# Sorting each node tile's expert choices with a one-hot product and storing them as eight runs, in place of two indirect scatters

## The reference, cut to what matters

```python
N, D, H, E = 12500, 256, 512, 8                      # 212500 edges
msgs = layernorm(x)[src] * edge_weight[:, None]
agg  = segment_sum(msgs, dst, N)                     # dst is sorted
x    = x + agg @ W.T + b
xf   = layernorm(x)
probs = softmax(xf @ gate_w + gate_b)
top2_vals, top2_idx = top_k(probs, 2)
for e in range(E):                                   # weight is zero unless e was chosen
    out += cw[:, e] * (gelu(xf @ W1[e] + b1[e]) @ W2[e] + b2[e])
x = x + out
```

## Time and profile before

| | us |
|---|---|
| median of 3 runs (2953.14 to 2955.53) | 2954.43 |
| the profiled execution | 2958.51 |
| its span | 2956.7 |
| POOL busy in the span | 2013.2 |
| PE busy in the span | 2196.5 |
| DVE busy in the span | 1409.3 |

### The profile page before, as it was taken

The page is one execution under the profiler, slowest core; times in us unless marked ns, Lnnn a source line. Parts: engine busy times, 40 slices in busy tenths (PEclk is TensorE's granted clock), DMA queues, the critical chain, the costliest instruction groups (busy, mean ns, idle before and its releaser), DMA issues.

```text
span 2956.7 us, 40846 instructions
## 1 busy us (share of the span) xinstructions
PE 2196.5 (74%) x9206; PEld 1482.4 (50%) x9207; DVE 1409.3 (48%) x5982; ACT 740.5 (25%) x1985; POOL 2013.2 (68%) x2107
## 2 busy tenths in 40 slices
PE   3656755984876977966966877978877887776695
PEld 2433533653654655644644654655555555544463
DVE  8855434453453443453454453443555555454422
ACT  3410200330221332321321221322322222222242
POOL 6657777777777777777777777777777777751121
PEclk8777977897988988988988987989998899887798
DMA  9663433443444443445555444434455564542423
GB/s 337 225 237 115 127 116 115 136 126 121 129 139 123 133 126 122 139 147 163 173 165 163 145 131 132 132 118 125 138 168 161 161 194 148 158 131 85 151 86 109
DMA packets 231445, 432.24 MB, mean 146 GB/s; under 512 B 47020, under 2 KB 158542, under 8 KB 228006
## 3 DMA queue, kind: packets, MB, share of 16 engines
q0 software_dynamic: 100368, 275.72, 31.3%
q1 hardware_dynamic: 128246, 144.38, 15.4%
q10 hardware_dynamic: 2592, 9.45, 0.8%
HBM read 326.80 MB, written 102.56 MB: 145 GB/s over the span
## 4 chain that ended last, share of the span: by engine, by line
POOL 50%; issue 20%; PE 15%; DVE 11%; DMA 3%; ACT 1%; ACTq 1%; DVEq 0%; SPq 0%; POOLq 0%
POOL rows L363 40%; POOL slots L391 5%; PE bank L599 5%; POOL results L396 5%; PE bank L685 4%; PE bank L667 3%; DVE spread L976 1%; DMA results<-y_sb,result_i 1%; PE bank L676 1%; DMA got<-results 1%; DVE y_sb L1154 1%; DVE item_t L1124 1%; DVE square_n L1023 1%; DVE pre_bn L932 1%; DVE bn L955 0%
## 5 line engine op out<-in xcount | busy, mean ns | idle before, releaser
L363 POOL DMA_INDIRECT rows<-xhat,src_t x1536 | 1470.0, 957 | 476.4 <-issue 464.4
L599 PE MATMUL bank<-rows,spread 128*80 128x256 f32 x3328 | 910.2, 435 | 324.8 <-issue 160.1
L599 PEld LDWEIGHTS bank<-rows,spread 128*80 128x80 f32 x3328 | 564.1, 175 | 607.6 <-issue 320.4
L685 PE MATMUL bank<-w,hT 128*128 x1848 | 489.1, 411 | 115.3 <-ACT hT L822 66.9
L685 PEld LDWEIGHTS bank<-w,hT 128*128 128x128 f32 x1848 | 366.2, 205 | 229.1 <-issue 180.9
L667 PE MATMUL bank<-w,xiT 128*128 x924 | 452.0, 612 | 11.6 <-ACT xiT L805 2.2
L989 DVE TENSOR_TENSOR acc<-acc,bank 128x160 f32 x208 | 67.0, 322 | 755.4 <-PE bank L589 730.3
L396 POOL DMA_INDIRECT results<-y_sb,result_i x231 | 226.8, 982 | 237.4 <-DVE y_sb L1157 181.3
L976 DVE TENSOR_SCALAR spread<-iota_w,dst_rel,wgt 128x80 f32<-128x80 f32 x1536 | 378.5, 340 | 0.2
L1153 DVE CAST result_i<-xi 128x1 int32 x231 | 35.1, 152 | 620.6 <-PE bank L685 339.1
L822 ACT ACTIVATE hT<-bank,b1T 128x128 f32<-128x128 f32 x924 | 263.4, 367 | 217.8 <-PE bank L676 212.2
(11 more groups left out here) (159 smaller groups left out, 1755.3 us busy)
## 6 DMA issues: line engine op xcount, KB each, us to landing
xi<-slots SPq DMA_DIRECT2D x231, 136.0 KB, 2.7
got<-results SPq DMA_DIRECT2D x97, 256.0 KB
rows<-xhat,src_t POOLq DMA_INDIRECT x1536
x_t<-in_x SPq DMA_DIRECT2D x97, 128.0 KB
x_d<-x_t SPq DMA_DIRECT2D x97, 128.0 KB, 2.3
res<-x_d SPq DMA_DIRECT2D x97, 128.0 KB
out_nodes<-res SPq DMA_DIRECT2D x97, 128.0 KB
w<-in_x SPq DMA_DIRECT2D x12, 1024.0 KB, 12.7
```

What stands on the lines that cost most here:

```text
L363: pool.indirect_dma_start(rows[q][:, c, :], None, x if g < RAW else xhat, bass.IndirectOffsetOnAxis(ap=src_t[:, g * CG + c:g * CG + c + 1] ...
L599: done = nc.tensor.matmul(B_SUM[0:W, 0:D], spread[g % 2][:, c, :], rows[q][:, c, :], start=c == 0, stop=c == CG - 1)
L685: done = nc.tensor.matmul(B_Y[:, 0:D], hT[i % 2][:, j, :], w2[:, bass.ds(e, 1), j, :].rearrange("p o f -> p (o f)"), start=j == 0, stop=j ...
```

## The change

POOL no longer sends. For each tile, in the turns after its part is placed:

1. DVE (`mask_choices`, at the end of its turn) writes a one-hot matrix of 128 nodes by 256 places, where a place is the choice's rank when the tile's 256 choices are sorted by expert.
2. PE (`sort`, a turn later) multiplies it with the tile in two products of 128 places by 272 columns. They go to the bank that `linear` uses, the first behind `turn_sums`, the second behind `step_down`. ACT copies each out (`copy_sorted`), and `linear`, now behind `step_down`, waits for the second copy.
3. SP (a turn later) stores the 256 sorted rows in a staging array in DRAM (`store_sorted`).
4. SP (a turn later) loads sixteen addresses into registers at once and copies eight runs of 128 rows each, one for an expert, from staging to `slots` (`copy_runs`). A run is always 128 rows long, and what lies behind its end is overwritten by the next tile's run, so a tile's copies wait for those of the tile before.

`place` has five more small operations for the run starts, and loses the cast to `slot_i`. The ring of node sums falls from 16 tiles to 8. `xs` is cleared at the start. One tile in a turn is masked, in place of two or four sent; three items in a turn start once the last run is planned. The plan grows from 235 to 239 turns. By turn 150, 107 items have entered it where 116 had; by turn 207, when the last group is gathered, 186 where 192 had. The last tile is done in turn 222 where it was sent in turn 219.

```diff
-RING = 16
+RING = 8
+STAGE = 3 * P
+STAGES = 3
...
-        for _ in range(2 if busy else 4):
-            if send_next < NT and place_at.get(PART_OF[send_next], tau) < tau:
-                t.sends.append(send_next)
...
+        if turns:
+            t.sort, t.stage, t.runs = turns[-1].mask, turns[-1].sort, turns[-1].stage
+        if send_next < NT and place_at.get(PART_OF[send_next], tau + 1) <= tau:
+            t.mask = send_next
+            send_next += 1
+        if t.runs >= 0 and t.runs == PARTS[PART_OF[t.runs]][1] - 1:
+            sent_at[PART_OF[t.runs]] = tau
...
+            def store_sorted(t):
+                if t >= STAGES:
+                    sp.wait_ge(runs_in, 16 * NX * (t - STAGES + 1))
+                sp.wait_ge(sorted_ready, 2 * t + 2)
+                sp.dma_start(stages[t % STAGES][0:2 * P].rearrange("(h p) f -> p h f", p=P), sorted_x[t % 2][:]).then_inc(staged[t % STAGES], 16)
...
+                at = loaded_row(sp, run_ends[k % 2][:, j].rearrange("p c e -> p (c e)"))
+                sp.wait_ge(staged[t % STAGES], 16 * (t // STAGES + 1))
+                if t:
+                    sp.wait_ge(runs_in, 16 * NX * t)
+                if t in EPOCH_TILES[1:]:
+                    sp.wait_ge(tails_in, 16 * NX * EPOCH_OF[k])
+                for e in range(NX):
...
+                    sp.dma_start(slots[bass.ds(b, P), :], stages[t % STAGES][bass.ds(a, P), :]).then_inc(runs_in, 16)
...
+            def sort(t, h):
+                if h == 0:
+                    pe.wait_ge(mask_set, t + 1)
+                pe.wait_ge(x1_ready, n_linear[0])
+                if t or h:
+                    pe.wait_ge(sorted_ready, 2 * t + h)
+                nc.tensor.matmul(B_NODE[:, 0:XW], sort_mask[t % 2][:, h * P:(h + 1) * P], xs[:, t % XR, :],
+                                 start=True, stop=True).then_inc(sort_done, 1)
...
+            def copy_sorted(t, h):
+                act.wait_ge(sort_done, 2 * t + h + 1)
...
+                nc.scalar.activation(sorted_x[t % 2][:, h, :], B_NODE[:, 0:XW], ACT.Copy).then_inc(sorted_ready, 1)
...
+            nc.vector.memset(xs[:], 0.0)
...
+                nc.vector.tensor_scalar(first_choice[:], iota_s[:], at[0], None, op0=ALU.is_equal).then_inc(half_mask, 1)
+                dve.wait_ge(half_mask, t + 1)
+                nc.vector.scalar_tensor_tensor(sort_mask[t % 2][:], iota_s[:], at[1], first_choice[:],
+                                               op0=ALU.is_equal, op1=ALU.add).then_inc(mask_set, 1)
```

More of the change, by code:

```diff
@@ L119 @@
     refill: int = -1
-    sends: list = field(default_factory=list)
+    mask: int = -1
+    sort: int = -1
+    stage: int = -1
+    runs: int = -1
     steps: list = field(default_factory=list)
@@ L230, in build @@
     xhat = nc.dram_tensor("xhat", (N, D), F32, kind="Internal").ap()
+    stages = [nc.dram_tensor(f"stage{i}", (STAGE, XW), F32, kind="Internal").ap() for i in range(STAGES)]
     blocks = slots.rearrange("(n p) f -> n p f", p=P)
@@ L325, in tile, with loaded_row @@
             return acc[:, :, t % RING * P:(t % RING + 1) * P]
+        def loaded_row(eng, row):
+            return nc.values_load_multi_w_load_instructions(row, engines=(eng.engine,), skip_runtime_bounds_check_because="bounded where used")[1]
         def valid_rows(t):
@@ L385, in _ @@
             pool.wait_ge(src_rest, 16)
[L387 to L392, removed]
             def scatter_result(i):
@@ L527, in turns @@
                         refill(t.refill)
+                    if t.stage >= 0:
+                        store_sorted(t.stage)
+                    if t.runs >= 0:
+                        copy_runs(t.runs)
+                        k = PART_OF[t.runs]
+                        if t.runs == PARTS[k][1] - 1 and ends_epoch(k):
+                            fill_tails(k)
                     if t.load_x >= 0:
@@ L706, in turns @@
                         turn_sums(t.add)
+                    if t.sort >= 0:
+                        sort(t.sort, 0)
                     if t.gate >= 0:
                         turn_node(t.gate)
+                    for a, _, c, _ in t.steps[:1]:
+                        step_down(a, c)
+                    if t.sort >= 0:
+                        sort(t.sort, 1)
+                        n_sorted[0] = t.sort + 1
                     if t.linear >= 0:
                         linear(t.linear, fast)
[L711 to L712 removed]
                     if t.gate >= 0:
@@ L841, in turns @@
                         step_up(a, b)
+                    if t.sort >= 0:
+                        copy_sorted(t.sort, 0)
                     if t.gate >= 0:
@@ L848, in turns @@
                             copy_xiT(c)
+                    if t.sort >= 0:
+                        copy_sorted(t.sort, 1)
                     if t.softmax >= 0:
@@ L1201, in turns @@
                         place(t.place)
+                    if t.mask >= 0:
+                        mask_choices(t.mask)
                     for a, _, _, _ in t.steps[1:]:
```

82 lines of the change are left out of this document (59 added, 23 removed).

## The result

The changed kernel takes 2984.18 us (median of 4 runs, 2983.01 to 2989.02) where the kernel before takes 2954.81 beside it: a ratio of 1.0098, 95% interval 1.0086 to 1.0111. It is slower by 1%. The forecast was 2923 and faster; the time lies in its range. The profiled execution took 2989.02 us, its span is 2987.3, so that 30.6 us of span are to be explained.

The account below looks back on a forecast made before the run. POOL was taken to bound the long middle, with the PE-ACT-DVE chain close behind and pacing the third stretch along with POOL. Start 0, middle -112, third stretch +26 and end +55 gave -31 on 2954.4: 2923 us, range 2845 to 3035.

Parts of the forecast that it names:

- SP's nine DMAs ... nothing: SP's store and eight copies a tile: under 8.56 us in a turn of 11, late issues needed later, cost nothing.
- Eight copies "less" with one register load: SP's issue time a tile: less than the 8.56 us of eight stores with a register load before each.
- The middle, -112: Long stretch with parts of eight tiles, 368 to 1960 us before the change: falls from 1592 to 1480 us.
- POOL's floor: POOL's time in the long middle: 1592 less 146.5 for sends, less 12 for nine later items, 1434 us.
- The mask, 4 us net a part: Turn after `place`: PE waits for DVE's mask, written after the item list; bounds 1 and 9 us, 4 taken.
- second rival: Sort's hand-overs: mask's wait costs 5 us more a part, second copy holds `linear` 1.5 us; 3019 us, chance 0.28.
- `linear`'s wait, 0.9 us: PE's `linear` waits for ACT's second sorted copy every second tile: between 0 and 2 us, 0.9 taken.
- The copies' bytes, 20 us in the middle: 784 copies of 136 KB, 0.44 us each of all 16 DMA engines: 20 us added between 368 and 1960 us.
- third rival: Copies load the DMA engines and SP's queue, or SP's issue makes items late: 150 for 20, 3053 us, chance 0.12.
- The end, +55: Stretch after the last gather: later last tile 19, three items 13, six tiles 5, mask waits 8, 8 and 2 us.
- The third stretch, +26: Small parts, 1960 to 2643 us before the change: PE's chain goes from 683 to 709 us, POOL's floor not reached.
- The rule on headroom: Weight-load share gives PE half its time free; as a rival, POOL alone bounds: 2793 us, chance 0.12.

Follow-up runs that it names:

- pool_back: The changed kernel with POOL also scattering a constant tile twice, into arrays nobody reads, in each turn with a mask: 3111.97 us, 1.0542 of the kernel before.

## Why the prediction was wrong

- **"SP's nine DMAs ... nothing"** is the step that failed. I had compared one tile's 8.56 us with a turn of 11 and looked for who needs the next item. The right sum is of SP's whole turn: 1.6 us of register load, 6.2 of copies, and for x tile, item, output, the two result loads, x1 and staging store some 3 more. That is nearly a whole turn of 11.4 us, so that in copy turns SP's stream became a pacing engine beside PE and POOL. PE's wait for items rose from 15.3 to 94.6 us, and relieving SP of three copies took 36 us off with the later tail stores, of the 61 by which the forecast missed. Where the other 25 went stays open. The 2984 lie in the stated range, but that is its width and no credit: the sign was wrong.
- **Eight copies "less" with one register load**: right, but by 0.8 us only. They took 6.2 us and the load 1.6 more, together 7.8 against 8.56.
- **The middle, -112**: -64. POOL's floor was right: its groups come to 1431.6 us there, busy and issue, against my 1434, and PE's wait for rows fell to 50.4 us in this stretch, under the 60 named. But 96 us of POOL's idle time were no issue; I had allowed 25 + 20 for the interplay and the copies.
- **The mask, 4 us net a part**: by the one test, too much. The wait came much as predicted, 21 times and 13.3 at most. The sum holds 74 us for it (32 + 24 + 18), and putting the first mask ahead of the list gives 12 back, 0.7 a part. What DVE's two operations and the products cost in themselves was not measured on an undisturbed chip. The second rival (9 us a part, chance 0.28) is refuted as far as the mask's place goes: it named the right sign and the wrong place.
- **`linear`'s wait, 0.9 us**: 0.58, 38 times.
- **The copies' bytes, 20 us in the middle**: perhaps too little. Twice the bytes cost 92 us over the whole, in part by SP's waits; what the first helping cost was not measured. The third rival, at 0.12, held the mechanism of SP's issue time and late items, but its 3053 is 69 us too high. I gave it the smallest chance because "rows wait a turn in their buffers", which holds for rows and not for items.
- **The end, +55**: +70. The items behind the tails (17.57 us at 2812.9) were not in it.
- **The third stretch, +26**: +36. 30.6 us of PE's wait for items lie there:

```profile
PE bank L705 <- DMA xi<-slots: 30.6, 9, 9.8
```

- **The start, 0**: -11. Sends freed more there than half of their time.
- **The last gather near 2557**: it ends at 2603.9 (it starts at 2602.99 and takes 0.95), just past the 2600 that I had named as proof against me.
- **The rule on headroom** (the Trainium skill, Perfetto Trace Analysis, "Identifying the Most-Contended Engine") would have given 2793. No run came near it, with PE's weight-load share at 50% before and 52% after. My own argument against it was loose, though: of the 257 us that I called waits on ACT and DVE, 68.6 are "issue" and 13.5 are for items.
- **The rule on issuers** (the Trainium skill, DMA: Bandwidth & Descriptors, "Issuing engines are not separate DMA queues"): another issuer saves the time to initiate. The traces agree: POOL's time came back, and `pool_back` puts it at 133 us, its bytes included. The same section calls that time "usually small relative to the DMA itself". Here it is not: SP needs 0.8 us to issue a copy whose bytes I had put, as an estimate, at 0.44 us of the 16 engines, and doubled issues cost five times what doubled bytes cost.

## What to carry to other kernels

An engine that is idle in every table of busy time can still be full for a stretch: count its issues, register loads and waits for a whole turn, all steps, and set that sum against the turn, before work is moved to it. Test a suspected queue by doubling its issues at equal bytes; if the time follows by most of the added microseconds, there was no room. That does not say what relief will bring: here three copies fewer on SP shortened a copy turn by 0.2 us, since POOL and PE were next. And a long wait in the list is worth only what the next wait leaves of it: 108 us of the mask's wait were worth 12.

## What the runs showed of the hardware that I had not expected

- A copy from DRAM to DRAM at register addresses takes SP 0.8 us from one to the next, 12.37 to 12.87 us for sixteen in the stretch shown. It is the same for 64, 128 or 256 rows (6.12 to 6.55 us for eight of 256 rows near 1550 us). Most of SP's other issues in the same turns show 0.34 to 0.52, single ones up to 1.40.
- The load of sixteen registers on SP took 0.97 to 3.14 us, 1.6 in the median.
- ACT issues the same copies no slower, eight in 5.87 to 6.81 us and three in 2.06 to 2.28.
- The kernel before took 3690 to 3697 us in three sessions and 2950 to 2956 in all others, one chip among both, with POOL's gathers at the same 957 ns and late hand-overs. The cause is open. Ratios of kernels differed between the conditions: 0.981 to 0.990 there and 0.994 on an undisturbed chip for the same pair.
